# SwiGLU units of a fused feed-forward kernel: where the two second products stand between the first ones

## The reference

```python
# layer 1 (Taylor-like attention replacement, and a SwiGLU feed-forward)
approx_up = hidden_states @ up_w.T ; gate_pre = hidden_states @ gate_w.T
...                                   # six powers of (gate_pre - point), each times approx_up @ fuse_weight[:, :, i].T
ffn_out = jax.nn.silu(hidden_states @ ffn_gate_w.T) * (hidden_states @ ffn_up_w.T) @ ffn_down_w.T
x = _layernorm(x + approx_out + ffn_out)
# layer 2 (sparse feed-forward: of each block of 32 hidden units one is picked)
inter = x @ c1_w.T @ c2_w.T                       # 512 -> rank 16 -> 1792
idx = argmax(inter in blocks of 32)               # 56 picks a token
h = relu(w1[idx] . x) ; out = sum(h * w2t[idx])
x = _layernorm(x + out)
```

## Time and profile before

| | |
|---|---|
| median of 3 runs | 713.79 us (713.75 to 713.9) |
| profiled execution | 714.67 us, of which the span of the trace is 712.9 us |
| PE busy | 704.6 us, 99% of the span |
| DVE busy | 527.2 us, 74% |
| ACT busy | 269.5 us, 38% |
| POOL busy | 291.0 us, 41% |
| mean granted clock of PE | 0.998 of full speed |

### The profile page before, as it was taken

One profiled execution on the slowest core, in us unless ns is written; L12 is line 12 of the kernel. 1 busy time (PEld: TensorE's weight loads), 2 busy tenths in 40 slices (PEclk: granted clock), 3 DMA queues, 4 the chain that ended last, 5 costly groups with the idle time before them and its releaser, 6 DMA issues.

```text
span 712.9 us, 10308 instructions
## 1 busy us (share of the span) xinstructions
PE 704.6 (99%) x3949; PEld 380.7 (53%) x3949; DVE 527.2 (74%) x977; ACT 269.5 (38%) x455; POOL 291.0 (41%) x276
## 2 busy tenths in 40 slices
PE   9999999999999999999999999999999999999996
PEld 3444444444444444444444456666666666667763
DVE  5989897796887778677787988958885778337235
ACT  1575457435721121221222234444334333443342
POOL 0462443211111161244215576897366435743331
PEclk9999999999999999999999999999999999999999
DMA  9546309401000110110010222121224101220101
GB/s 338 251 145 195 60 15 378 81 14 46 2 15 17 22 22 2 28 27 20 6 16 19 50 50 50 29 66 17 49 75 64 47 4 60 62 46 1 60 2 60
DMA packets 40545, 44.67 MB, mean 63 GB/s; under 512 B 25008, under 2 KB 32816, under 8 KB 39600
## 3 DMA queue, kind: packets, MB, share of 16 engines
q1 hardware_dynamic: 37808, 39.29, 18.6%
q0 software_dynamic: 2112, 4.19, 3.3%
q10 hardware_dynamic: 576, 0.52, 0.2%
HBM read 34.33 MB, written 4.42 MB: 54 GB/s over the span
## 4 chain that ended last, share of the span: by engine, by line
PE 85%; issue 1%; DVE 1%; ACT 1%; POOL 1%; DVEq 0%; ACTq 0%
PE acc L545 31%; PE pb L525 15%; PE pa L525 15%; PE pb L791 10%; PE pa L791 8%; PE acc L631 2%; PE acc L880 2%; PE pick_b L697 1%; PE pick_a L697 1%; POOL big L1160 1%; PE pick_a L682 0%; ACT work L1120 0%; PE pick_b L880 0%; PE pick_b L541 0%; PE acc L541 0%
## 5 line engine op out<-in xcount | busy, mean ns | idle before, releaser
L545 PE MATMUL acc<-big,work 128*128 128x512 f16 x1038 | 235.1, 379 | 0.0
L1151 POOL TENSOR_TENSOR work<-work 128x512 f16<-128x512 f32 x90 | 107.6, 1206 | 273.7 <-ACT work L1023 213.7
L545 PEld LDWEIGHTS acc<-big,work 128*128 128x128 f16 x1038 | 101.6, 98 | 115.4
L525 PE MATMUL pa<-xs,big 128*128 128x512 f16 x480 | 111.2, 379 | 0.0
L525 PE MATMUL pb<-xs,big 128*128 128x512 f16 x480 | 110.1, 379 | 0.0
L1890 DVE TENSOR_TENSOR pa<-pa,big 128x512 f32<-128x512 f32 x28 | 19.6, 699 | 79.6 <-ACT big L1103 68.6
L525 PEld LDWEIGHTS pa<-xs,big 128*128 128x128 f16 x480 | 46.1, 98 | 54.1
L525 PEld LDWEIGHTS pb<-xs,big 128*128 128x128 f16 x480 | 46.0, 98 | 53.4
L631 PE MATMUL acc<-big 128*128 128x512 f16 x328 | 72.0, 379 | 0.2
L1023 ACT ACTIVATE work<-work 128x512 f16<-128x512 f32 x40 | 25.3, 631 | 111.0 <-DVE work L1617 111.0
L1160 POOL TENSOR_TENSOR big<-work,big 128x512 f16<-128x512 f32 x27 | 36.7, 1375 | 63.3 <-ACT big L961 63.1
(11 more groups left out here) (235 smaller groups left out, 988.1 us busy)
## 6 DMA issues: line engine op xcount, KB each, us to landing
big<-in_w_all SPq DMA_DIRECT2D x2, 3840.0 KB, 18.0
big<-in_x_t SPq DMA_DIRECT2D x16, 256.0 KB, 6.3
rows<-in_x POOLq DMA_DIRECT2D x4, 1024.0 KB, 12.0
big<-spread_rows SPq DMA_DIRECT2D x16, 256.0 KB, 6.1
big<-in_w_all SPq DMA_DIRECT2D x2, 1536.0 KB, 11.4
big<-spread_rows SPq DMA_DIRECT2D x16, 192.0 KB, 5.1
out<-rows SPq DMA_DIRECT2D x3, 1024.0 KB, 4.4
big<-in_w_all SPq DMA_DIRECT2D x1, 2048.0 KB, 14.6
```

Source lines behind the costliest of these rows:

```text
L525: mm = nc.tensor.matmul(dst[:, :], weights(wp)(kc * P, P), x_part16(g, xp, kc), start=(kc == 0 and wp == xp), stop=(kc == KC - 1 and wp == 1))
L545: mm = nc.tensor.matmul(acc[t][:, :], act_part(pair, j, ap, t * P, P), weights(wp)(0, H), start=(first and ap == wp), stop=(last and ap == 1))
L1151: nc.gpsimd.tensor_tensor(act_part(pair, j, 1), act32[j], act_part(pair, j, 0), ALU.subtract).then_inc(act_lo, halves)
```

## The change

In the SwiGLU units from (1,1) on, the second product of the unit before's chunk 0 moves ahead: it now stands behind the first chunk's up product. That of chunk 1 stays behind the second chunk's up product. Score 3 stands behind that. Units (g, 0) of groups 2 and 3 are changed likewise; group 0 and unit (1,0) keep the old order. No instruction is added or removed on any engine, and only PE's order changes.

```diff
-            def unit1(g, u, tile=None, own=None, start=False, converted=False, after_gate=None):
+            def unit1(g, u, tile=None, own=None, start=False, converted=False, after_gate=None, halfway=None):
...
                     split_product(pb, lambda part: w1_part(s, 1, part), g).then_inc(up_ready, 1)
+                    if halfway is not None and j == 0:
+                        halfway()
                     if tile is not None and j == 1:
                         scores(tile, 2, pick_a)
 
-            def down(g, u, kind, scored=None):
+            def down(g, u, kind, scored=None, js=range(2)):
...
-                for j in range(2):
+                for j in js:
...
-                    if j == 0 and scored is not None:
+                    if j == 1 and scored is not None:
                         scores(scored, 3, pick_b)
...
-                unit1(g, 1)
-                down(g, 1, "first")
+                unit1(g, 1, halfway=lambda: down(g, 1, "first", js=(0,)))
+                down(g, 1, "first", js=(1,))
                 for u in range(2, U1):
-                    unit1(g, u, t(u - 1), (g - 1, u - 2))
-                    down(g, u, "middle", t(u - 1))
+                    unit1(g, u, t(u - 1), (g - 1, u - 2), halfway=lambda: down(g, u, "middle", js=(0,)))
+                    down(g, u, "middle", t(u - 1), (1,))
...
-                unit1(g + 1, 0, g * TPG - 1, (g - 1, TPG - 1))
-                down(g + 1, 0, "last", scored=g * TPG - 1)
+                unit1(g + 1, 0, g * TPG - 1, (g - 1, TPG - 1), halfway=lambda: down(g + 1, 0, "last", js=(0,)))
+                down(g + 1, 0, "last", g * TPG - 1, (1,))
```

## The result

| | before | after |
|---|---|---|
| median | 714.06 us (713.75 to 714.28, 6 runs) | 717.12 us (715.88 to 719.22, 6 runs) |
| ratio, 95% interval | | 1.0048 (1.0032 to 1.0064) |
| profiled execution | 714.67 us, span 712.9 | 715.88 us, span 714.1 |
| PE busy | 704.6 us | 704.1 us |

The changed kernel is slower by 0.5%; 717.1 us was forecast. Its executions also spread more widely, over 3.3 us and not over 0.5 (over 1.8 us in 29 later executions of the kernel before), which no part of the prediction speaks of.

A forecast was written before the change was run, and what follows sets the result against it. The prediction took PE, busy 99% of the span, as the bound. It added four waits, 0.27 + 0.45 + 0.45 + 2.15 = 3.3 us, to 713.79 for 717.1 us; range 714.4 to 718.7 us.

The forecast's parts named there:

- Nothing to win on PE: PE in the SwiGLU phase, groups 1 to 3: no wait there for the reorder to remove, so no gain; faster 0.03.
- Everything of scores 0 to 2 comes 2.59 us later, the reader doesn't: Per unit, DVE's work on scores 0 to 2 starts 2.59 us later; the next unit's first up product doesn't move.
- The boundary: End of unit (3,4): PE's first `pb` product of the sparse phase waits for the swiglu product, 2.15 us.
- the first rival: No stop by POOL in the new places; only the boundary waits, 0.74 us, total 714.5 us; chance 0.10.
- The three up products: Up products behind (2,2), (1,4) and (2,4) wait because POOL's L1232 stops rank_hits 2: 0.27, 0.45 and 0.45 us.
- The zeros: Cost 0: units with scores and no job, (3,2) and (3,3) (up to 0.2), banks in (g,1), the transposes.
- Rival 3: A further wait, from late transposes in (2,2), (3,2) or up products in (3,3), (3,4): 0.5 to 1.5 us; chance 0.12.
- The sum: The four forecast waits of PE, 0.27 + 0.45 + 0.45 + 2.15 = 3.3 us; bounds 0.74 and 4.5.
- Rivals 1 and 2: No stop of rank_hits 2 by POOL: in all four units, 714.5 us, chance 0.10; at boundary alone, 715.7 us, chance 0.12.
- Rival 4: The wait doesn't show at all, some of the stretch being less tight than it reads: 713.8 us; chance 0.05.

## Why the prediction was right, and where not

- **Nothing to win on PE: right.** The kernel with the swiglu product moved ahead has all the reordering and no wait, and takes the same time (1.0002) as the kernel before.
- **Everything of scores 0 to 2 comes 2.59 us later, the reader doesn't: right**, from the PE rows of the changed trace.
- **The boundary, forecast 2.15 us: right.** 1.95 us in one trace, 2.18 to 2.20 in four (the second of the changed kernel, three of the kernel with only the last unit changed). As forecast, rank_hits 2 is stopped until 0.25 us after the end of POOL's long instruction, so it is POOL that sets the wait. The run with that instruction out of the way leaves 1.32 us: the 0.74 of DVE's queue that the first rival gives, and 0.57 from rank_hits 0, which meets another instruction of POOL's. The first rival names such a stop, the sum has none. Which of the two waits comes hangs on that meeting. In the changed kernel's first trace POOL's L1214 starts at 417.83 and rank_hits 0 at 417.84, and DVE is the one held up. In its second trace it is the other way round:

```profile
418.54 0.39 DVE L1752 TENSOR_TENSOR big<-big,rev_wide 128x448 f16<-128x448 f16 x1
...
418.55 0.97 POOL L1214 TENSOR_TENSOR quad<-quad 128x256 f32<-128x256 f32 x1
```

  Here POOL's instruction takes 0.97 us instead of 0.72, L1234 starts 6.18 us after score 0 and not 5.94, and the wait is 2.20 us and not 1.95.
- **The three up products, forecast 0.27, 0.45 and 0.45: right in place and sign, too large in the latter two.** Measured 0.15, 0.27 and 0.28, taking (2,2) first. POOL's long instruction came earlier than I had it: in (2,2) it started 8.35 us after score 0 before, which with the shift of 2.59 would be 5.76; measured are 306.79 - 301.17 = 5.62. POOL met one product of rank_hits less on its way: its two additions of L1206 take 1.29 us there, and the same two took 1.44 in the kernel before (L1204), where rank_hits 0 fell on them. That it "doesn't move" was wrong by 0.14 us, on a wait of 0.27.
- **The zeros: right.** Up products in units without a job, in (3,2) and (3,3), the banks in (g,1) and the transposed rows in (2,2) and (3,2) show no wait. Rival 3 didn't come about.
- **The sum, 3.3 us: measured 3.1 and 3.3 in two sets, but not by these terms alone.** The waits make 2.65 to 2.9 us in the traces. The clock, a term that was not in the sum, comes on top in some executions. It is shown in two traces of the kernel with only the last unit changed (1.6 us each), and in three of the changed kernel's executions by their mean clock; in none of the changed kernel's own two traces did it fall. That it makes up the 0.2 to 0.6 us between the waits and the medians is likely and not shown: one execution of 717.38 us has a mean of 0.999, which leaves no room for it. So the number's closeness is in part luck, by two errors of opposite sign: small waits 0.5 us too large together, and the clock missing. The range, 714.4 to 718.7, held the median but not the slowest executions, 719.2.
- Rivals 1 and 2 (no stop by POOL) are refuted: rank_hits 2 takes 1.01 to 1.65 us beside L1234 and 0.39 without it. Rival 4 (no wait at all) is refuted by the same traces.

## What to carry to other kernels

When the bounding engine has no gaps, as here, a reorder on it alone has no wait to remove and can only add some. What it loses is set by the smallest margin of any reader behind it: list each wait of that engine, how much later its producer's queue now starts, and what is in that queue ahead of the producer. Look at phase boundaries for themselves; the five units with scores and no job of POOL's kept 0.8 us to spare, and the last unit, whose reader sits 1.3 us behind it and not 2.8, had three quarters of the waiting. A product that PE waits for should stand ahead of bookkeeping on its engine; moving it ahead of one pick made the same order free.

## What the runs showed of the hardware

**A short wait of PE can cost again through the clock.** Behind 2.2 us without a matmul, after hundreds of microseconds of dense matmuls, the granted clock of a stretch of 5 us fell to 0.66 and 0.67 in two traces, and stayed full in three others with a wait of 1.95 to 2.2 us and in one with 3.4; six matmuls of 256 columns then took 1.1 to 1.3 us instead of 0.66. The price was 1.6 us, and 2.2 us behind a wait of 4.2. Behind 1.3 us (11 executions) no mean under 0.998 was seen, and nine of the eleven had 0.999 or more. A wait of one size gave times in two clumps: the seven executions of the kernel with only the last unit changed took 715.3 and 716.0, or 717.2 to 718.1 us. A wide spread of executions was the first sign of it. Why the clock falls in one execution and not in the next, no run here shows.

**The port between DVE and POOL.** A product of two fp16 rows in SBUF took 0.39 us alone, and where POOL's instruction had started first it ended 0.25 us after that one (products of 2.25, 1.65, 1.01 and 0.96 us). Where DVE started first, by 0.01 us, POOL's took 0.97 us instead of 0.72. The Trainium skill's "SBUF — State Buffer", section "Who interferes with whom", has this as a lock held for the whole instruction; the runs agree, on either side of the lock, and moving POOL's long instruction took 1.3 us or more off the kernel's waits (2.65 to 2.9, against 1.32).
